# Searching a top-k threshold in two alternating groups of tiles, woven into the quantisation of feed-forward weights

## What is computed

```python
def A(x, ctx, Wq, Wk, gamma_raw):              # ctx: (4, 512, 128)
    Q, K = heads(ctx @ Wq.T), heads(ctx @ Wk.T)          # 4 heads
    sim = einsum('bhnd,bhmd->bnm', Q, K) / (sqrt(32.) * 4)
    k = int(512 * 0.3)                                   # 153
    threshold = top_k(sim, k)[0][:, :, -1:]              # the k-th largest of a row
    A_l = sigmoid(sim) * (sim >= threshold)
    A_l = (A_l + swapaxes(A_l, -1, -2)) * 0.5
    g = sigmoid(gamma_raw)
    return (1 - g) * layernorm(x) + g * A_l
x = x + tanh(g_xattn[0]) * A(...)

def q_w(w):            # blocks of 32 along the last axis
    scale = 2 ** (floor(log2(max|w| of the block)) - 2)
    e = exponent of w / scale, at least 0
    return clip(round(w / scale / 2**(e - 1)) * 2**(e - 1), -6, 6) * scale
def B(x, w_gate, w_up, w_down):
    lin = lambda x, w: q_act(x) @ q_w(w).T
    return lin(silu(lin(x, w_gate)) * lin(x, w_up), w_down)
x = x + tanh(g_ffn[0]) * B(layernorm(x), ...)
```

## Time and profile before

| | us |
|---|---|
| median of 3 runs | 2155.13 (2154.55 to 2155.16) |
| profiled execution | 2153.45 |
| its span, first to last instruction | 2151.7 |
| of this: search, 40.25 to 269.50 | 229.25 |
| last count, to 276.70 | 7.20 |
| masking, to 311.20 | 34.50 |
| weight stage, to 509.10 | 197.90 |
| norm(0) starts | 515.39 |
| DVE busy in the span | 1576.6 (73%) |
| ACT busy | 959.3 (45%) |
| PE busy | 1449.3 (67%) |

### The profile page before, as it was taken

The page is one execution under the profiler, slowest core; times in us unless marked ns, Lnnn a source line. Parts: engine busy times, 40 slices in busy tenths (PEclk is TensorE's granted clock), DMA queues, the critical chain, the costliest instruction groups (busy, mean ns, idle before and its releaser), DMA issues.

```text
span 2151.7 us, 32048 instructions
## 1 busy us (share of the span) xinstructions
PE 1449.3 (67%) x10939; PEld 922.7 (43%) x11014; DVE 1576.6 (73%) x2526; ACT 959.3 (45%) x1591; POOL 426.4 (20%) x325
## 2 busy tenths in 40 slices
PE   4000051113767776889999770999999999999990
PEld 2000040012333332444444370677777777777760
DVE  4999999997888887888888453466666666666634
ACT  5787811123232223555545332455555555555520
POOL 3000003243000000666767606000000000000006
PEclk8555575556888887999999855899999999999995
DMA  9000030100000000000000007666666666666617
GB/s 354 9 0 0 0 118 0 78 0 25 0 0 0 0 0 0 2 1 2 2 2 1 2 0 273 226 227 233 227 225 232 227 226 229 229 227 229 228 61 234
DMA packets 86470, 222.09 MB, mean 103 GB/s; under 512 B 7424, under 2 KB 7680, under 8 KB 85888
## 3 DMA queue, kind: packets, MB, share of 16 engines
q1 hardware_dynamic: 80752, 204.37, 27.8%
q0 software_dynamic: 5120, 16.78, 2.3%
q10 hardware_dynamic: 528, 0.02, 0.0%
HBM read 184.44 MB, written 36.70 MB: 103 GB/s over the span
## 4 chain that ended last, share of the span: by engine, by line
PE 47%; DVE 7%; issue 4%; POOL 2%; ACT 0%; DMA 0%; POOLq 0%; DVEq 0%; ACTq 0%; SPq 0%
PE PS L1527 23%; PE PS L1546 11%; PE PS L1164 3%; DVE R L1017 2%; PE PS L1140 2%; PE PS L1150 2%; PE PS L1125 2%; DVE R L989 2%; PE PS L1139 1%; POOL R L1696 1%; PE PS L1412 1%; PE PS L1507 1%; PE PS L1115 1%; PE PS L1404 1%; DVE R L1021 1%
## 5 line engine op out<-in xcount | busy, mean ns | idle before, releaser
L1527 PE MATMUL PS<-R 128*128 128x256 f16 x4416 | 499.1, 273 | 1.1 <-ACT R L1583 1.1
L1527 PEld LDWEIGHTS PS<-R 128*128 128x128 f16 x4416 | 431.8, 98 | 66.8 <-issue 1.4
L1546 PE MATMUL PS<-R 128*128 128x512 f16 x1104 | 253.3, 379 | 0.2 <-DVE R L1656 0.2
L1234 DVE SCALAR_TENSOR_TENSOR R<-wring,R 128x1024 f16<-128x1024 f32 x184 | 221.3, 1223 | 27.5 <-ACT R L1229 24.3
L1092 ACT ACTIVATE R<-PS 128x512 f32<-128x512 f32 x256 | 151.6, 597 | 160.4 <-PE PS L1140 157.1
L989 DVE TENSOR_REDUCE R<-PS 128x1 f32<-128x512 f32 x256 | 167.4, 685 | 49.5 <-PE PS L1125 48.0
L399 ACT ACTIVATE R<-R 128x512 bf16<-128x512 f32 x256 | 181.0, 708 | 45.1 <-DVE R L443 45.1
L1229 ACT ACTIVATE R<-wring 128x1024 f16<-128x1024 f32 x184 | 188.9, 1050 | 23.8 <-DMA wring<-in_L_ffn_w_kernel_dram 21.3
L833 PE MATMUL PS<-R 128*128 128x512 bf16 x495 | 143.0, 439 | 78.1 <-DVE R L769 59.8
L1696 POOL DMA_INDIRECT R<-slot_out,posi x32 | 34.0, 1061 | 764.5 <-DMA slot_out<-R 755.1
L1648 DVE SCALAR_TENSOR_TENSOR R<-PS,R 128x512 f32<-128x512 f32 x92 | 63.5, 690 | 165.6 <-ACT R L1596 165.6
(11 more groups left out here) (221 smaller groups left out, 2508.9 us busy)
## 6 DMA issues: line engine op xcount, KB each, us to landing
wring<-in_L_ffn_w_kernel_dram SPq DMA_DIRECT2D x138, 512.0 KB, 4.3
R<-in_L_ffn_w_kernel_dram SPq DMA_DIRECT2D x46, 512.0 KB, 4.6
wring<-in_L_ffn_wo_kernel_dram SPq DMA_DIRECT2D x46, 512.0 KB, 5.1
R<-in_L_ffn_wo_kernel_dram SPq DMA_DIRECT2D x46, 512.0 KB, 5.0
slot_rows<-R SPq DMA_DIRECT2D x1, 11776.0 KB, 41.1
R<-slot_rows SPq DMA_DIRECT2D x23, 512.0 KB, 4.2
slot_out<-R SPq DMA_DIRECT2D x23, 512.0 KB, 3.0
X<-in_x_dram SPq DMA_DIRECT2D x4, 1024.0 KB, 9.0
```

What stands on the lines that cost most here:

```text
L1234: nc.vector.scalar_tensor_tensor(out=lo, in0=raw[c % RING], scalar=WSCALE, in1=hi, op0=ALU.mult, op1=ALU.subtract).then_inc(cut_lo, 1)
L1527: mm = nc.tensor.matmul(bank[2 * (j % 2) + m][:, g * SLOT:(g + 1) * SLOT], w[:, at:at + P], z[:, pz * 1024 + k * SLOT:pz * 1024 + (k + 1) ...
L1546: mm = nc.tensor.matmul(bank[6 + t], src[:, c * SLOT + t * P:c * SLOT + (t + 1) * P], w[:, at:at + D], start=(c == 0 and src is IH and pw ...
```

## The change

The 16 tiles form two groups of 8, and each search step becomes two halves, h even for tiles 0 to 7 and h odd for tiles 8 to 15. The buffer `marks` (8 tiles of bfloat16) takes the place of `junk`; counts no longer come from accumulators.

- ACT marks 7 tiles of a half by Sign, DVE one (`mark`, a comparison less 0.5, which PE weighs double with `ident_2`).
- PE (`pe_search`) adds the marks by matmuls with the identity, 8 matmuls of 64 columns of each tile summed into one bank: 8 x 256, 8 x 64 and 8 x 192 columns a half. DVE sums the 64 left (`tally`).
- DVE keeps `near`, the key with the next bit already flipped, so that a candidate is one operation behind the comparison; bits come from a table of 32 memsets.
- After each of the first 60 halves DVE does one of five parts of a weight unit (`dve_weights`), the multiplication by the inverse scale now among them. PE transposes a finished unit each five halves, ACT copies it.
- All 16 tiles get the last count. A now overwrites SIM; WGU is filled while the search runs.
- The keys of C come one batch ahead of each masking batch on PE, in banks 6 and 7; masking has 6 banks in place of 8. POOL has no weight work.
- SP asks for six weight units at the start and for each further one when a buffer is free.

The diff, cut to its core (removed lines stand in the kernel above):

```diff
+        def pe_apply(pe):
+            pe.wait_ge(wtr_sb, 25)
             for b in range(NB):
+                pe_keys(pe, b)
                 pe.wait_ge(a_ready, b * TPB + TPB)
                 a = A[:, b * 2048:(b + 1) * 2048]
                 for i in range(TPB):
-                    to = bank[4 * (b % 2) + i]
-                    if b >= 2:
-                        pe.wait_ge(x1_done, (b - 2) * TPB + i + 1)
+                    tile = b * TPB + i
+                    to = bank[tile % 6]
+                    if tile >= 6:
+                        pe.wait_ge(x1_done, tile - 5)
...
         def act_search(act):
             act.wait_ge(sim_sb, NT)
...
+            for h in range(HALVES):
+                act.wait_ge(cand_ready, h + 1)
+                for j in range(ACT_MARKS):
+                    tile = h % 2 * HALF + j
+                    if j % 4 == 0 and h:
+                        act.wait_ge(fold_ps, 2 * h - 1 + j // 4)
+                    nc.scalar.activation(marks[:, j * S:(j + 1) * S], SIM[:, tile * S:(tile + 1) * S], ACT.Sign,
+                                         bias=cfloat[:, tile:tile + 1], scale=-1.0).then_inc(marked, 1)
+                if h >= 6 and (h - 6) % 5 == 0 and (h - 6) // 5 < 11:
+                    act_weights(act, (h - 6) // 5)
+            act_weights(act, 11)
+            act.wait_ge(raw_used, 12)
...
+            for b in range(NB):
+                act_key_parts(act, b)
+                act_keys(act, b)
...
+        def pe_search(pe):
+            pe.wait_ge(id_ready, 2)
+            pe.wait_ge(sim_sb, NT)
+            for h in range(HALVES + 2):
+                def fold(tiles, weight):
+                    lo, hi = tiles
+                    for c in range(8):
+                        mm = nc.tensor.matmul(bank[4 + h % 2][:, lo * 64:hi * 64], weight,
+                                              marks.rearrange("p (t m) -> p t m", m=S)[:, lo:hi, c * 64:(c + 1) * 64],
+                                              start=(c == 0), stop=(c == 7))
+                    return mm
+
+                for q in range(2):
+                    if h < HALVES:
+                        pe.wait_ge(marked, h * ACT_MARKS + (ACT_MARKS if q else 4))
+                        if q:
+                            pe.wait_ge(marked_dve, h + 1)
+                    else:
+                        pe.wait_ge(marked_dve, HALVES + (h - HALVES) * HALF + 4 * q + 4)
+                    if q and h < HALVES:
+                        fold((7, 8), ident_2)
+                        mm = fold((4, 7), ident_b[:])
+                    else:
+                        mm = fold((4 * q, 4 * q + 4), ident_b[:])
+                    mm.then_inc(fold_ps, 1)
+                if h >= 5 and h % 5 == 0 and h <= 60:
+                    pe_weights(pe, h // 5 - 1)
 
...
+            nc.vector.tensor_scalar(ident_2, ident_b[:], 2.0, None, ALU.mult).then_inc(bit_step, 1)
+            v.wait_ge(bit_step, 36)
+            nc.vector.tensor_copy(gone, key).then_inc(cand_ready, 2)
+
+            def tally(h):
+                v.wait_ge(fold_ps, 2 * h + 2)
+                nc.vector.tensor_reduce(cnt[:, h % 2 * HALF:h % 2 * HALF + HALF],
+                                        bank[4 + h % 2].rearrange("p (t m) -> p t m", m=64), AX, ALU.add).then_inc(tallied, 1)
+                v.wait_ge(tallied, h + 1)
+
+            def mark(h):
+                t = h % 2 * HALF + HALF - 1
+                v.wait_ge(cand_ready, h + 1)
+                if h:
+                    v.wait_ge(fold_ps, 2 * h)
+                nc.vector.tensor_scalar(marks[:, (HALF - 1) * S:], SIM[:, t * S:(t + 1) * S], cfloat[:, t:t + 1], 0.5,
+                                        ALU.is_lt, ALU.subtract).then_inc(marked_dve, 1)
+
+            def search(h):
+                n, g = h // 2, slice(h % 2 * HALF, h % 2 * HALF + HALF)
+                tally(h)
+                nc.vector.tensor_scalar(keep[:, g], cnt[:, g], float(S - 2 * TOPK), -1.0, ALU.is_le,
+                                        ALU.mult).then_inc(keep_step, 1)
+                v.wait_ge(keep_step, h + 1)
...
+                v.wait_ge(near_step, h - 1)
+                if n < 31:
+                    nc.vector.scalar_tensor_tensor(out=cbits[:, g], in0=keep[:, g], scalar=bit[:, n:n + 1], in1=near[:, g],
+                                                   op0=ALU.bitwise_and, op1=ALU.bitwise_xor).then_inc(cand_ready, 1)
+                nc.vector.scalar_tensor_tensor(out=key[:, g], in0=keep[:, g], scalar=bit[:, n:n + 1], in1=key[:, g],
+                                               op0=ALU.bitwise_and, op1=ALU.bitwise_xor).then_inc(key_step, 1)
+                v.wait_ge(key_step, h + 5)
...
+            mark(0)
+            for u in range(12):
+                for k in range(5):
+                    mark(5 * u + k + 1)
+                    search(5 * u + k)
+                    dve_weights(v, u, k)
+            for h in range(60, HALVES):
+                if h + 1 < HALVES:
+                    mark(h + 1)
+                search(h)
+
...
+            for h in range(HALVES, HALVES + 2):
+                for j in range(HALF):
+                    t = h % 2 * HALF + j
+                    if j % 4 == 0:
+                        v.wait_ge(fold_ps, 2 * h - 1 + j // 4)
+                    nc.vector.tensor_scalar(marks[:, j * S:(j + 1) * S], SIM[:, t * S:(t + 1) * S],
+                                            cfloat[:, t:t + 1], None, ALU.is_ge).then_inc(marked_dve, 1)
+            tally(HALVES)
+            tally(HALVES + 1)
+            nc.vector.tensor_scalar(keep, cnt, float(TOPK), -1.0, ALU.is_ge, ALU.mult).then_inc(fin_step, 1)
+            nc.vector.tensor_tensor(flip, key, cand, ALU.bitwise_xor).then_inc(fin_step, 1)
...
         def act_key_parts(act, b):
-
-            act.wait_ge(kt_ps, b * 2 + 1)
+            if b:
+                act.wait_ge(kt_ps, b * 2)
+            else:
+                act.wait_ge(fold_ps, 2 * HALVES + 4)
+            if b:
+                act.wait_ge(klo, b * 2)
             for n in (0, 2):
                 nc.scalar.copy(parts(cks, n), heads(C[:, bass.ds(b * 512, 512)])).then_inc(khi, 1)
...
+        def sp_weights(sp):
+            for u in range(12):
+                if u >= 6:
+                    sp.wait_ge(raw_used, u - 3)
+                if u < 8:
+                    src = (w_gate, w_up)[u // 4][u % 4 * 512:(u % 4 + 1) * 512, :].rearrange("(t p) h -> p t h", p=P)
+                    sp.dma_start(raw_unit(u).rearrange("p (t h) -> p t h", h=D), src).then_inc(raw_in[raw_slot(u)], 16)
+                else:
+                    sp.dma_start(raw_unit(u), w_down[(u - 8) * P:(u - 7) * P, :]).then_inc(raw_in[raw_slot(u)], 16)
...
+        def dve_weights(v, u, k):
             n = UNIT // BLK
+            raw_u = raw_unit(u)
+            wf = lambda c: v.wait_ge(wf_step, u * 4 + c)
+            wq = lambda c: v.wait_ge(wq_step, u * 4 + c)
+            if k == 0:
+                v.wait_ge(raw_in[raw_slot(u)], raw_loads(u))
+                if u:
+                    v.wait_ge(wb_ready, u)
                 nc.vector.tensor_reduce(wam, blocks(raw_u), AX, ALU.max, apply_absolute_value=True).then_inc(wf_step, 1)
+                wf(1)
                 nc.vector.tensor_scalar(wpow.bitcast(I32), wam.bitcast(I32), EXPONENT, None,
                                         ALU.bitwise_and).then_inc(wf_step, 1)
+                wf(2)
+                nc.vector.tensor_scalar(wsc, wpow, TINY, 0.25, ALU.max, ALU.mult).then_inc(wf_step, 1)
+                wf(3)
+                nc.vector.reciprocal(wri, wsc).then_inc(wf_step, 1)
+            elif k == 1:
+                wf(4)
+                nc.vector.tensor_tensor(blocks(wy), blocks(raw_u), spread(wri, n), ALU.mult).then_inc(raw_used, 1)
+                v.wait_ge(raw_used, u + 1)
+                nc.vector.tensor_scalar(wc.bitcast(I32), wy.bitcast(I32), EXPONENT, None,
                                         ALU.bitwise_and).then_inc(wq_step, 1)
+            elif k == 2:
+                wq(1)
                 nc.vector.tensor_scalar(wc, wc, 1.0, 1.5 * 2.0 ** 22, ALU.max, ALU.mult).then_inc(wq_step, 1)
+                wq(2)
+                nc.vector.scalar_tensor_tensor(out=wy, in0=wy, scalar=6.0, in1=wc, op0=ALU.min,
                                                op1=ALU.add).then_inc(wq_step, 1)
+            elif k == 3:
+                wq(3)
+                nc.vector.tensor_tensor(wy, wy, wc, ALU.subtract).then_inc(wq_step, 1)
+            else:
+                wq(4)
+                if u:
                     v.wait_ge(wtr_ps, 2 * u)
+                nc.vector.scalar_tensor_tensor(out=blocks(wb), in0=blocks(wy), scalar=-6.0, in1=spread(wsc, n),
                                                op0=ALU.max, op1=ALU.mult).then_inc(wb_ready, 1)
...
+            for b in range(NB):
+                pool_keys(pool, b)
             pool_selectors(pool)
 
         def pool_selectors(pool):
+            pool.wait_ge(a_ready, NT)
```

(8 more changed lines are left out.)

262 lines of the change are left out of this document (77 added, 185 removed).

## The result

The changed kernel takes 2044.21 us, median of 4 runs (2041.38 to 2047.04); the kernel before took 2154.84 beside it (4 runs). The ratio is 0.9492, 95% interval 0.9472 to 0.9513. The profiled execution took 2041.38 us for a span of 2039.2.

A forecast was written before the change was run, and what follows sets the result against it. Search and weight stage were taken as paced by DVE, with waits in the old search. norm(0) at 411.5 for 515.4 takes 103.9 off 2153.45, giving 2049.6; with 1.7 for the median, 2051, range 2040 to 2088.

The forecast's parts named there:

- DVE's search part of a half: DVE's mark, tally and small operations in each half of a search step: 1.83 us, with the mark at 0.36.
- ACT's mark: Each of ACT's seven marks in a half was taken as 0.526 us, with bounds 0.526 and 0.707.
- last four halves: The end of the search, after the halves with weight parts, goes at ACT's pace: 12.5 us.
- slow clock, in the search: TensorE runs at high clock for most of the search; 4 us were added for the rest.
- last count: The count over all 16 tiles after the search: 9 us at high clock, 11.7 at low, for 7.2 before.
- T2 to norm(0): From the last count's end (T2), masking with its keys, then POOL's power, to the first feed-forward ACT pass: 45.5 us.
- rival (b): An operation costs its upper bound: Sign at 0.707 gives 2080, DVE's mark at 0.68 gives 2071; chance 0.20.
- above 0.75: Sign that the prediction holds: TensorE's granted clock stays above this share between 60 and 350 us.
- Rival (a): TensorE stays at 1.2 GHz, with DVE waiting some 0.8 in one half of five: 2063; chance 0.20.
- Rival (c): POOL's subtractions and DVE's masks block each other in masking: 13 us more, 2064; chance 0.07.
- Rival (d): The search's folds on TensorE don't pipeline, each matmul costing 0.312: 222 us more, 2273, slower than before; chance 0.03.
- Rival (e): Marks or weights do not overlap at all and the change only reorders: within 0.2% of the old time; chance 0.01.

The follow-up runs named there:

- The probe: Changed kernel plus fifteen more ACT passes of 512 elements, three of each of five forms, ahead of the sigmoids behind the search; one run, 2047.38 us.
- the last version: Changed kernel with two weight units loaded ahead of the zeros, dummy TensorE matmuls, and POOL's first key subtractions put in DVE's idle time; 2036.48 us.

## Why the prediction was right, and where it was off

The mechanism held: the search, with DVE and ACT waiting for each other, and the weight stage, bound by DVE, became one stage in which DVE and ACT are both full. Term by term:

| term | predicted | measured |
|---|---|---|
| first candidate | 41.5 | 41.2 |
| first half | 6 | 6.4 |
| wait for unit 0 | 3 | 3.06 |
| DVE's search part of a half | 1.83 | 1.87 |
| five halves and a unit | 24.2 | 23.9 |
| sixty halves with twelve units | 290 | 287.5 |
| ACT's mark | 0.526 (to 0.707) | 0.622 |
| last four halves | 12.5 | 14.6 |
| slow clock, in the search | 4 | nothing in the middle |
| end of the search, T1 | 357 | 352.8 |
| last count | 9 | 12.9 |
| T2 | 366 | 365.6 |
| T2 to norm(0) | 45.5 | 41.0 |
| norm(0) | 411.5 | 406.6 |
| behind norm(0) | as before | 3.7 less, spread |

- **DVE's price per half** was right, since it was taken pass by pass from rows 3 to 6 (only the mark, an estimate, came at 0.40 for 0.36); the L694 and L698 passes at 1.23 and 1.22 confirm that the 4.54 in rows 5 was POOL's doing. The unit's cadence is the starts of L682, 53.03 to 316.10 over 11 units.
- **ACT's mark was mis-sized.** The step "sixteen Sigmoids of the same size took 8.41, I take 0.526" compared a pass without a bias column with one that has it. The bound above, 0.707, was the Sign with accumulator. The probe shows 0.62 for the very form. In the sixty halves with weights it cost nothing, only because 7 x 0.62 + 0.38 of copies is 4.73, just under DVE's 4.8. In the last four, which the text itself puts at ACT's pace, it did cost: 28 marks of 0.096 more are 2.7, and these halves took 14.6 for 12.5, with DVE waiting 1.88, 2.83 and 3.37 for folds. The text called DVE the bound with ACT at 4.1; in fact there was no slack, which the run without the subtraction shows.
- **The balance was luck.** Nothing in the rows priced a mark of this form. At the bound of 0.707 rival (b) would have come and its own sum gives 2080; at 0.622 ACT stays just under DVE. One more mark on ACT costs 25 us (2069.9), one less 20 (2064.7).
- **The clock.** "High clock for most of it" was half right: 0.73 of full speed in the middle, 0.92 in the last halves and 0.62 in the last count (0.78 in the middle when the same kernel ran again, so the sign "above 0.75" told nothing). Rival (a)'s condition was half fulfilled, but its price of 0.8 in one half of five was not: DVE waited 0.2 us in 280. TensorE kept busy gained 2 to 3 us in the whole kernel.
- **The last count, 9 for 12.9.** 1.9 of it is the two small operations held by POOL, which the text had weighed only for the masks; the two variants without this hold take 11.4 and 11.5 from the last keep to the first mask for 13.3. Of the other 2.0 the slow clock is at most some 0.3, though the granted clock was 0.63 here and the text's 11.7 at low clock lies close: with TensorE kept busy in the search it was 0.83 in the same operations, and the last count took 12.6 all the same. The marks come every 0.40, not 0.36, which is 0.6 in sixteen, and DVE waits 0.40 and 0.61 for folds; the rest was not traced further.
- **Masking, 45.5 for 41.0**, failed in the step "casts 1.2 + POOL 4.7 + transposes 1.9 from 1.9 before T2" in two terms. POOL's two subtractions took 2.26, not 4.7. In rows 8 they ran beside DVE's passes; with DVE standing still they took 2.27 in the last version, so the 4.69 held some 2.4 of waiting, which the text had priced as work. And the casts began 3.8 before T2, not 1.9, because POOL's hold on the two small operations lay between: the hold that lengthened the last count also covered the keys. With only one of the two the keys would have come at T2 + 3.6 or later by these numbers, behind the masks. So the keys were on time, and the matmuls began 2.8 behind T2, as before the change, not 6. Nor did the two last batches take 1.3 more: the batches stand 7.95 apart, which is the 0.9 + 7.0 of the text.
- **Rival (c)**, the masks held by POOL, cost 0.9 in a batch (3.63 for four masks, 2.73 without) and all of it was hidden behind TensorE, as the text had it. The lock was real; it bit in other places than the one watched.
- **Rival (d)**: 24 matmuls of a half with two changes of weights took 1.89 + 0.61 + 1.47 = 3.97 at half clock, so they are pipelined. The row that it took its 312 ns from had said so: 192 transposes were busy 22.6 us in all, 0.118 each, and 312 is how long one of them lasts while the next ones run. Its limit of 0.245 per matmul is also off; with its own 0.4 and 0.5 it is (6.55 - 0.9) / 24 = 0.235. **Rival (e)** is what the variant with the weights behind the search is, and there the kernel is 2.2% slower, not the same.

Up to T1 the 4 us for the slow clock were not needed and the units took 2.5 less, while the last four halves took 2.1 more: 4.2 too long. Behind T1 two errors, 3.9 in the last count and 4.5 in masking, went against each other, which is luck. So the sum came out 5 us too long at norm(0). The rest to the 7 us is the spread behind it.

## What to carry to other kernels

When two stages need the same engine most and leave others idle, move work of one stage off that engine, even if this stage alone gets slower by it (282 us for 229 here), and put the other stage's work in its place; groups that take turns give the time in which it fits. Then price every engine's share of one turn with rows of the very form (pointer operand, accumulator, type, length), since the balance is decided by hundredths of a microsecond and the next engine takes over at once. A small DVE operation on SBUF in the critical chain should not start while POOL's passes run, as it can be held until POOL's pass ends: put POOL's passes into a wait of DVE, not on a moment when POOL happens to be free. And before a release is moved earlier, read which one comes last at the waiting instruction; here the keys were already there.

## What the runs showed of the hardware

- A bias column adds 0.092 us to an ACT pass of 512 elements, for Sign and Sigmoid and for float32 and bfloat16 output, in the forms run: 0.706 for 0.614, and 0.62 for 0.526 from start to start.
- A POOL pass of 3.72 us stretched a DVE operation on eight elements from 0.172 to 2.89; the length of the hold is what is left of POOL's pass, not a share of the DVE operation. A reduction out of PSUM beside it kept its 0.69.
- The same two POOL subtractions took 2.26 to 3.35 us from the last count on and 4.69 before: a duration of POOL beside a busy DVE holds its waits too.
- The granted clock of a stretch with TensorE busy two thirds of the time was 0.73 to 0.79 in runs of the same search; filling its gaps took it to 0.96. 2236 matmuls instead of 1586 were then issued in those 280 us, and the time barely moved.
